# Edges issued ahead of the halo ring, a patch-layout scratch image, and image loads from GpSimd's queue

## The reference, cut to what matters

```python
def step(u, _):                                   # 10 steps on x: (8, 16, 512, 512) f32
    ux, uy, uxx, uxy, uyy = _derivs(u)            # Sobel, and Sobel of Sobel; each clipped to +-10
    g2 = ux * ux + uy * uy
    K = jnp.clip((uxx * uyy - uxy * uxy) / ((1 + g2) ** 2 + EPS), -5.0, 5.0)
    H = jnp.clip(((1 + uy * uy) * uxx - 2 * ux * uy * uxy + (1 + ux * ux) * uyy) / (2 * denH ** 3 + EPS), -5.0, 5.0)
    u = u + DT * jnp.clip(alpha * K + beta * H, -1.0, 1.0)
    return jnp.pad(u[:, :, 1:-1, 1:-1], ((0, 0), (0, 0), (1, 1), (1, 1)), mode='edge'), None
x = 0.7 * u + 0.3 * x                             # layer 0
out = conv3x3(relu(conv3x3(x, w1) + b1), w2) + b2 + x   # layer 1, 16 channels
```

## Time and profile before

| | |
|---|---|
| median of 3 runs | 40605.43 us (40586.49 to 40609.12) |
| the profiled execution | 40599.69 us, span 40597.9 us |
| layer 0 | from about 380 to about 36930 us of the span |
| layer 1 | from about 36930 us to the end |
| busy, share of the span | PE 86%, DVE 84%, ACT 82%, POOL 50% |
| matmul clock granted, mean | 0.971 of full speed |
| transfer engines busy (16) | 57% |

### The profile page before, as it was taken

How to read it: one execution, slowest core, us unless ns; L and a number is a source line. 1 busy time by engine, 2 the same in 40 slices (tenths; PEclk the granted TensorE clock), 3 DMA queues, 4 the chain that set the end, 5 groups by cost and what they waited for, 6 DMA issues and landing times. The chain is left out here.

```text
span 40597.9 us, 445411 instructions
## 1 busy us (share of the span) xinstructions
PE 34779.5 (86%) x120896; PEld 22578.0 (56%) x120896; DVE 34223.0 (84%) x31730; ACT 33168.8 (82%) x33722; POOL 20444.4 (50%) x7685
## 2 busy tenths in 40 slices
PE   5888888888888888888888888888888888888999
PEld 3555555555555555555555555555555555554444
DVE  8999999999999999999999999999999999994111
ACT  5888889888888889888888889888888889885333
POOL 3555555555555555555555555555555555551000
PEclk9999999999999999999999999999999999999999
DMA  7555556555555555555555556555555556554333
GB/s 181 79 78 79 79 75 76 77 79 79 79 79 79 79 74 76 77 79 79 78 78 79 79 74 77 77 79 78 79 79 79 78 76 76 77 78 88 99 99 97
DMA packets 2728323, 3335.51 MB, mean 82 GB/s; under 512 B 2236356, under 2 KB 2236484, under 8 KB 2422212
## 3 DMA queue, kind: packets, MB, share of 16 engines
q1 hardware_dynamic: 2727364, 3324.78, 56.8%
HBM read 626.33 MB, written 301.47 MB: 23 GB/s over the span
## 5 line engine op out<-in xcount | busy, mean ns | idle before, releaser
L645 PE MATMUL tame_slot<-tame_split,tame_M 128*128 128x512 f32 x51200 | 15359.2, 422 | 5684.4 <-DVE tame_ux L516 3252.1
L645 PEld LDWEIGHTS tame_slot<-tame_split,tame_M 128*128 128x128 f32 x51200 | 9234.4, 192 | 11664.9 <-DVE tame_cross L516 3060.2
L645 PE MATMUL tame_slot<-tame_halo,tame_M 112*128 112x512 f32 x51200 | 14449.7, 404 | 0.0
L357 POOL TENSOR_TENSOR tame_split<-tame_U,tame_split 128x1024 fp32r<-128x1024 f32 x2560 | 6230.8, 2434 | 12957.1 <-ACT tame_split L392 12957.1
L645 PEld LDWEIGHTS tame_slot<-tame_halo,tame_M 112*128 112x128 f32 x51200 | 9855.4, 192 | 2544.4
L369 POOL TENSOR_TENSOR tame_ux<-tame_ux,tame_cross 128x1024 f32<-128x1024 f32 x2560 | 8063.4, 3150 | 436.3 <-POOL tame_ux L363 436.3
L363 POOL TENSOR_TENSOR tame_ux<-tame_ux,tame_uy 128x1024 f32<-128x1024 f32 x2560 | 6151.2, 2403 | 2695.9 <-DVE tame_uy L516 2695.9
L655 PE MATMUL tame_slot<-tame_uxy,tame_unit 128*128 128x512 f32 x10240 | 4962.0, 607 | 7.2 <-DVE tame_slot L539 7.2
L432 ACT ACTIVATE tame_slope<-tame_slope 128x2048 f32<-128x2048 f32 x2560 | 4894.9, 1912 | 0.0
L427 ACT ACTIVATE tame_slope<-tame_slope 128x1024 f32<-128x1024 f32 x2560 | 2717.5, 1062 | 2153.1 <-issue 2151.1
L558 DVE TENSOR_TENSOR tame_uyy<-tame_slot,tame_slope 128x1024 f32<-128x1024 f32 x2560 | 3135.7, 1225 | 1201.1 <-PE tame_slot L655 1189.8
(11 more groups left out here) (58 smaller groups left out, 36779.3 us busy)
## 6 DMA issues: line engine op xcount, KB each, us to landing
tame_halo<-tame_split SPq DMA_DIRECT2D x2560, 520.0 KB
tame_halo<-tame_split SPq DMA_DIRECT2D x2560, 260.0 KB
tame_halo<-tame_split SPq DMA_DIRECT2D x5120, 65.0 KB
xin<-mixed SPq DMA_DIRECT2D x672, 319.0 KB, 4.3
tame_U<-in_x SPq DMA_DIRECT2D x256, 512.0 KB, 3.7
tame_stage<-in_x SPq DMA_DIRECT2D x128, 1024.0 KB, 8.4
mixed<-tame_stage SPq DMA_DIRECT2D x1024, 128.0 KB, 2.5
out<-res SPq DMA_DIRECT2D x672, 192.0 KB
```

The lines of the kernel that those rows point to most:

```text
L357: nc.gpsimd.tensor_tensor(split_rows(c, 1), half_rows(c), split_rows(c, 0).bitcast(F32), ALU.subtract).then_inc(lo_ready, 2)
L645: last = nc.tensor.matmul(ps[name][:, b * BANK:(b + 1) * BANK], M[0:lanes, matrix, :], rows(c, part)[:, b * y:(b + 1) * y, :], start=(n < ...
```

## The change

Four things change at once:

1. In SP's queue the edges of half k - 2 are issued first in every period, and all eight ring transfers stand together behind them. `exchange` has no `part` any more.
2. Image loads (`load_half`, `load_stage`) are issued by POOL on its own queue, at the start of its period, ahead of its three tensor operations; their waits (`blended`, `stored`) go with them.
3. The scratch tensor `mixed` has the layout of the patches, (B, 16, C, 8, 2048), so an image is stored with one transfer of 8 KB rows instead of ten of 256 B pieces. For this `place` swaps even and odd columns.
4. Layer 1 loads such rows as 256 B pieces (two transfers where a unit crosses a multiple of 16 rows) without the wrapped ends; DVE makes these with two small copies a unit (`wrap`); the products become one matmul of 512 and four of 256 columns; the loop over units is written out.

```diff
 def place(c):
-    return c // 2 + c % 2 * (PC // 2)
+    return c // 2 + (1 - c % 2) * (PC // 2)
...
-            def exchange(i, j, part):
+            def exchange(i, j):
                 at = 0
-                for m, (first, step, n, shift) in enumerate(RING):
-                    if m // (len(RING) // 2) == part:
-                        sp.dma_start(...)
+                for first, step, n, shift in RING:
+                    sp.dma_start(...)
                     at += n
...
             def store(r, i):
-                for to, col, x0, n in ([(PX + k * PX, k, 0, PX) for k in range(PC)]
-                                       + [(1, PC - 1, 0, PX - 1), (PX + PC * PX, 0, 1, PX - 1)]):
-                    sp.dma_start(rows[:, :, to:to + n],
-                                 tile[place(col):P:PC, :, x0:x0 + n]).then_inc(stored[i % 2], 16)
+                image = mixed[bass.ds(r // (C // SLOTS), 1), :, bass.ds(r % (C // SLOTS) * SLOTS + i, 1), :, :]
+                sp.dma_start(image.rearrange("b r o g c -> (b r o) g c"), stage[i % 2][:, :]).then_inc(stored[i % 2], 16)
+
+            def period(t, k, kind, r):                       # SP
+                c = k - 2
+                if exists(kind, c):
+                    edge_columns(t, c)
+                    edge_rows(t, c)
+                if k % 2 == 0 and kind != "tail" and not (kind == "last" and k == CHUNKS - 2):
+                    sp.wait_ge(lo_ready, split_done(t, k - 5))
+                    sp.sem_inc(split_whole, 1)
+                    if not (kind == "first" and k == 0):
+                        sp.wait_ge(product[LAST_FIELD], done(t, k - 1))
+                    exchange((k + 2) % CHUNKS // 2, (k + 2) % 4 // 2)
+                c = k - 4
+                if exists(kind, c) and ends(kind, c) and c % 2:
+                    sp.wait_ge(blended, r * CHUNKS + (c % CHUNKS + 1))
+                    sp.sem_inc(image_done, 1)
+                    store(r, c % CHUNKS // 2)
...
+        @block.gpsimd
+        def _(pool):
+            def load_half(r, k):
+                pool.dma_start(half(k), x[...]).then_inc(x_in[k], 16)
+
+            def load_stage(r, i):
+                pool.wait_ge(stored[i % 2], r * 32 + (i // 2 * 16 + 16))
+                pool.sem_inc(stage_free, 1)
+                pool.dma_start(stage[i % 2][:, :], x[...]).then_inc(stage_in[i % 2], 16)
...
             def period(t, k, kind, r):                       # POOL
                 closing = kind in ("closing", "last")
                 c = k - 3
                 if exists(kind, c) and ends(kind, c):
-                    sp.wait_ge(blended, r * CHUNKS + (c % CHUNKS + 1))
-                    sp.sem_inc(stage_done, 1)
+                    pool.wait_ge(blended, r * CHUNKS + (c % CHUNKS + 1))
+                    pool.sem_inc(stage_done, 1)
                     if goes_on(kind, c):
                         load_half(r + 1, c % CHUNKS)
                 for i, there in ((0, closing and k == 0), (1, closing and k == 1), (2, closing and k == 6),
                                  (3, kind in ("opening", "tail") and k == 0)):
                     if there:
                         load_stage(r, i)
...
+            def wrap(b, u):                                  # DVE, layer 1; waits for the unit's loads
+                nc.vector.tensor_copy(t[:, 1:PX], t[:, HALF:HALF + PX - 1])
+                nc.vector.tensor_copy(t[:, PX + W:PX + W + PX - 1], t[:, PX + HALF + 1:PX + HALF + PX]).then_inc(
+                    x_wrapped, 1)
...
             def product(out_ps, weights, cols, src):
-                for dx in range(K):
-                    last = nc.tensor.matmul(out_ps, weights[:, dx, 0:cols], src[:, dx * PX:dx * PX + W],
-                                            start=(dx == 0), stop=(dx == K - 1))
+                nc.tensor.matmul(out_ps, weights[:, 1, 0:cols], src[:, PX:PX + W], start=True, stop=False)
+                for dx, half, at in ((0, 0, PX + HALF), (0, 1, 0), (2, 0, 2 * PX + HALF), (2, 1, PX)):
+                    last = nc.tensor.matmul(out_ps[:, half * HALF:(half + 1) * HALF], weights[:, dx, 0:cols],
+                                            src[:, at:at + HALF], start=False, stop=(dx == 2 and half == 1))
```

More of the change, by code:

```diff
@@ L372, in period @@
             def period(t, k, kind, r):
+                closing = kind in ("closing", "last")
+                c = k - 3
+                if exists(kind, c) and ends(kind, c):
+                    pool.wait_ge(blended, r * CHUNKS + (c % CHUNKS + 1))
+                    pool.sem_inc(stage_done, 1)
+                    if goes_on(kind, c):
+                        load_half(r + 1, c % CHUNKS)
+                for i, there in ((0, closing and k == 0), (1, closing and k == 1), (2, closing and k == 6),
+                                 (3, kind in ("opening", "tail") and k == 0)):
+                    if there:
+                        load_stage(r, i)
                 if exists(kind, k - 1):
@@ L377, in period @@
                     low(t, k - 3)
+            for k in range(CHUNKS):
+                load_half(0, k)
             for k in range(CHUNKS):
@@ L740, in residual_convolutions, with source, count @@
         WEIGHT_DMAS = 2 * NEW * (K + 1)
[L742 to L750 removed]
+        def source(u):
+            return xtop if u == 0 else xbottom if u == UNITS - 1 else xin[(u - 1) % BUFS]
+        def count(b, u):
+            return b * UNITS + (u + 1)
         @block.sync
@@ L791, in _ @@
[L791 to L800 removed]
+                for u in list(range(BUFS + 1)) + [UNITS - 1]:
+                    load(b, u)
@@ L801, in _ @@
+                for u in range(UNITS):
+                    store(b, u)
+                    if 1 <= u < UNITS - 1 - BUFS:
+                        load(b, u + BUFS)
             for j in range(2):
@@ L826, in hidden @@
                                          ACT.Copy).then_inc(hidden_ready, 1)
-            units(act, hidden)
+            with act.Fori(0, B) as b:
+                for u in range(UNITS):
+                    hidden(b, u)
         @block.vector
@@ new lines, in output @@
+            def output(b, u):
+                pe.wait_ge(hidden_ready, count(b, u) + 2)
+                pe.wait_ge(out_ready, count(b, u))
+                product(po[u % 2][0:NEW_P, :], W2, NEW_P, hid[u % 2]).then_inc(out_product, 1)
+            with pe.Fori(0, B) as b:
+                hidden(b, 0)
+                for u in range(1, UNITS):
+                    hidden(b, u)
+                    if u < UNITS - 1:
+                        output(b, u - 1)
+                output(b, UNITS - 2)
+                output(b, UNITS - 1)
```

199 lines of the change are left out of this document (74 added, 125 removed).

## The result

The changed kernel takes 43088.6 us (median of 4 runs, 43070.4 to 43097.3) against 40603.3 us (4 runs) before: 1.0612 of the time, 95% interval 1.0594 to 1.0631, or 2485 us more.

A forecast was written before the change was run, and what follows sets the result against it. DVE was taken to bound layer 0, nine tenths of the span, so only its waits count. Terms 2744 - 893 + 96 - 80 + 96 + 140 = +2103 on 40599.7 us gave 42,700 us; range 41,500 to 43,800.

The forecast's parts named there:

- Part 1b: Blend at image changes: edges issued earlier remove long waits for edge rows, leaving 2.0 us each for ACT; -893 us.
- Two of the signs: PE's waits for the halo ring: about 1000 or more of them, adding up to 2000 to 3500 us.
- Part 1a: Layer 0: ring issued 9.3 us later, 3.9 late; 2.45 us more a pair over 1120 pairs, +2744 us.
- 2 + 2 or 0 + 4: PE's ring waits in two successive pairs add up to 3.9 us, split evenly or all in one; mean 1.95.
- Part 2: POOL issuing image loads: waits for the store delay its additions in k = 6 and k = 0; +96 us.
- on SP the same waits disappear: Moving image loads to POOL removes their waits from SP's queue; no size given.
- Part 3: One store issue replaces ten: -80 us at k = 6; against it, the first ring after the last blend, +96 us.
- Part 4: Layer 1 on PE: 256-column matmuls at 0.238 us (ph) and 0.216 (po) make units 0.20 us longer; +140 us.
- The ring is hidden after all: Rival: with a ring of 18.6 us instead of 22.5 behind the edges, nothing is late; 39,960 us; chance 0.12.
- POOL's queue becomes the wait: Rival: each of twelve loads holds POOL's additions, and DVE, by 3.1 us; 1190 us more, 43,900 us; chance 0.12.

The follow-up runs named there:

- run 1: Changed kernel with SP's old order (large ring transfers, columns, corners, rows), the other three parts kept: 40233.4 us, 0.9903 of the kernel before.
- run 3: Changed kernel with the four corner transfers cut from 2080 to 65 values a partition (output incomplete): 39610.4 us, 0.9751 of the kernel before.
- run 5: Kernel before with one edit, the edges of half k - 2 ahead of all eight ring transfers: 43576.4 us, 1.0732 of the kernel before.
- run 9: Changed kernel with the four corner transfers issued by GpSimd on its own queue, edges still first on SP: 39703.9 us, 0.9777 of the kernel before.
- run 2: Changed kernel with the image loads back on SP's queue, edges still ahead of the ring: 43168.5 us, 1.0624 of the kernel before.
- run 4: Changed kernel with edges first only in the periods with a blend, SP's old order elsewhere: 40479.1 us, 0.9964 of the kernel before.
- run 8: Changed kernel with SP's old order and the image loads back on SP: 40477.6 us, 0.9968 of the kernel before.
- run 7: Changed kernel with SP's old order and the four corner transfers issued by GpSimd on its own queue: 40378.5 us, 0.9945 of the kernel before.
- run 6: Changed kernel with PE doing the four ring-free matmuls of its first product before waiting for the ring: 43010.2 us, 1.0592 of the kernel before.
- run 11: Changed kernel with the ring's four corner transfers issued ahead of the four large ones on SP: 43432.2 us, 1.0696 of the kernel before.

## Why the prediction was right, and where its terms were off

The forecast, 42,700 us, was 390 us too low; the time fell into its range, and the loss came by the mechanism that it named. Part 1b, the largest gain in the sum, did not come as forecast. Two of the signs were missed narrowly: 903 waits for the ring in place of 1000 or more, and 3551 us in place of at most 3500.

**Part 1a, the late ring.** Close in each number. The ring goes out 9.34 us later against the pair's start (9.3 forecast), is late by 3.6 to 3.7 us (3.9), in every second pair ("2 + 2 or 0 + 4": it is 0 + 4), and a low stretch of clock follows. A mid-round pair costs 2.41 us more, against 2.45; by the two lengths of pair, 1.8 of this is the wait (1.95 forecast) and 0.6 the slow clock (0.5). Runs 1, 3 and 5 show the cause from three sides: without the order, without the tail, and with the order alone. The term was counted over 1120 pairs, three of them a round outside k = 8 to 70. There it was k = 72 that I had wrong: +8.2 us, not 2.4. The ring that is issued there shares the engines with an x load of 1 MB, which I had put at 3 us a round behind the last blend (there, k = 4, the pair lost 4.1 us). In one round, with a ring issued at 19734.90:

```profile
19740.56 0.57 POOL L327 DMA_DIRECT2D tame_stage<-in_x  x1
19760.85 2.07 PE L633 MATMUL tame_slot<-tame_split,tame_M 128*128 128x512 f32 x4 [8.97 <-DMA tame_halo<-tame_split]
```

That ring takes 25.9 us, where others take 22.1.

**Part 1b, the edges earlier.** This is the term that failed: -893 forecast. The step was "of the four long waits only ACT's part stays, 2.0 us each". The wait for edge rows did go (1153.6 to 4.3 us), but the wait for ACT went from 256.5 to 948.0 us, up to 10.2 us at a time. The chain in one change of images of the changed kernel: SP issues a ring, POOL the load of a half while it is on its way, ACT waits for the load, and the scale behind it comes late.

```profile
13802.41 8.84 SPq L266 DMA_DIRECT2D tame_halo<-tame_split  x8
...
13810.25 0.57 POOL L321 DMA_DIRECT2D tame_U<-in_x  x1 [3.07 <-DVE tame_stage L504]
...
13828.20 1.06 ACT L380 ACTIVATE tame_split<-tame_U 128x1024 fp32r<-128x1024 f32 x1 [6.45 <-DMA tame_U<-in_x]
13831.87 1.04 ACT L446 ACTIVATE tame_stage<-tame_stage 128x1024 f32<-128x1024 f32 x1
...
13832.94 1.23 DVE L504 SCALAR_TENSOR_TENSOR tame_stage<-tame_U,tame_stage 128x1024 f32<-128x1024 f32 x1 [8.59 <-ACT tame_stage L446]
```

The load is issued at 13810.25 and ACT can split only at 13828.20, 18 us later. Before, such a load landed in 3.7 us (page of the kernel before, part 6, the median):

```profile
tame_U<-in_x SPq DMA_DIRECT2D x256, 512.0 KB, 3.7
```

The median of 10.7 in the changed kernel must not be set against it, for it stands between two groups. The odd halves' loads are issued 32 us after a ring and land in 3.6 to 4.0 us; the even halves' are issued 8 to 14 us after one and land in 11.6 to 17.4 us (medians of each half). Before, the same loads were issued 22 us or more after the ring, when it was complete. In run 1 the median is 10.7 too, with the odd halves at 11.6 us, and there ACT waits only 23.7 us for x. It is the ring that has moved into the even loads' way. With the tail gone, loads issued equally soon after a ring land in 6.5 to 8.4 us (run 3) and 8.5 to 9.9 us (run 9). The blend pairs gave 371 us, and not 893; in run 3 they give 28.8 us a round, about the 27.9 forecast, so what the term left out was the x loads. Run 2 shows that the lateness does not need GpSimd's queue, run 3 that it needs the long tail, run 4 that the same happens with the new order in these periods alone.

**Part 2, GpSimd's loads.** Wrong sign: +96 forecast, about -260 measured with the old order (run 8 against run 1) and, with the new one, -80 at most, which is hardly more than the noise (run 2). The sentence "on SP the same waits disappear" stood there without a number; it was the larger side. POOL does wait for the store (95.7 us in 62 waits), which is about the size that I feared. The Trainium skill ("SBUF — State Buffer", section "SBUF: two separate sides") warns of VectorE holding up GpSimd's writing of descriptors. No run shows such a cost for the changed kernel: run 2, which took the loads away from GpSimd, is no faster, and one issue of a half image takes GpSimd 0.53 to 0.86 us. What held GpSimd before the 1 MB loads of run 7 is open, and no run tells whether it was this.

**Part 3, the stores.** The -80 for the pair k = 6 is what run 8 shows: 29.3 to 26.8 us, 32 times. In the changed kernel the pair's own late ring hides most of it (28.8 us).

**Part 4, layer 1.** +140 forecast, +15 measured. The step was "behind loads of 0.19: 0.238 each". Two products of the changed kernel:

```profile
39799.48 1.02 PE L868 MATMUL po<-hid,W 128*96 128x512 f32 x2
39800.34 1.89 PE L870 MATMUL po<-hid,W 128*96 128x256 f32 x8
39802.07 1.02 PE L868 MATMUL ph<-xin,W 128*128 128x512 f32 x2
39802.93 1.89 PE L870 MATMUL ph<-xin,W 128*128 128x256 f32 x8
39804.65 1.02 PE L868 MATMUL po<-hid,W 128*96 128x512 f32 x2
```

Eight short matmuls take 1.73 us, 0.216 each, with either size of weights, which is the 0.214 of half a long one: the loads are hidden in full. Both products take 5.17 us against 5.15. The 0.238 of layer 0 was thus not the price of such a load; where it comes from is open. (The upper bound of this part adds up to 257 us, not 270.)

**The rivals.** *The ring is hidden after all* fell, and run 9 shows that its border was right: with a ring of 17.8 us, under the 18.6 that it asked for, nothing is late. Had I asked what would spread the tail, and not only whether the new order does, I would have found the better kernel before the measurement. *POOL's queue becomes the wait* fell with run 2; only run 7 shows a piece of it.

Of the rule of the Trainium skill that the prediction weighed, the other half now matters. The Trainium skill ("DMA: Bandwidth & Descriptors", section on why a DMA increments its semaphore by 16) says that a transfer which takes fewer than 16 engines gets the lowest-numbered ones when it comes from SP's kind of queue, and the next ones in turn, from a cursor, when it comes from GpSimd's. The fall from full to nothing in run 9, without a tail at a quarter, agrees; which engines they are, no run here shows.

## What to carry to other kernels

In this kernel a transfer of 4 partitions kept to few engines, and four of them in a row from SP shared the same ones, a quarter of all (0.24 of sixteen): sixteen partitions in four transfers set the end of a ring of 112 (22.8 us, against 16.3 with short corners). Look for a stretch in which the transfer engines are busy to a constant quarter; moving these transfers to another queue may be worth more than any order. When a wait is taken away by issuing something earlier, ask what is now issued later, and which load it will run beside; a wait that goes under one name may come back under another (run 4). And count a wait of PE with the clock behind it: shortening the wait (run 6) can be worth nothing.

## What was not expected of the hardware

- The same four corner transfers make the ring 22 to 23 us long from SP's queue and about 18 us from GpSimd's (17.8 in run 9, 18.7 in run 7); issuing them first on SP does not shorten it (22.6 us).
- After a wait of 2.45 us for the ring, with 1.2 us of work and 1.27 us of idling ahead of it, the clock was 0.50 and then 0.72 over two stretches of 3.4 us; after one whole idle time of 4.85 us it was 0.50 for one stretch only. But run 11, with whole idle times, has stretches of 6.8 us too (437 of 512), so they do not need the split.
- Weight loads of 0.163 and 0.190 us hide behind matmuls of 256 columns, which start 0.216 us apart.
- A half image of x issued 8 to 14 us after a ring from SP landed in 11.6 to 17.4 us; issued 32 us after one, in 3.6 to 4.0 us.
- GpSimd idled up to 13.5 us before it issued a 1 MB load (run 7), with no releaser in the profile.
